# A two-layer graph kernel on one Trainium2 core: four second-layer tiles of each batch computed as halves, with copies loaded by GpSimd's queue, and the bias added by a DMA

## The reference

```python
# layer 0, attention
h = einsum('bnf,fo->bno', x, W)
e = h @ a1 + swapaxes(h @ a2, 1, 2);  e = where(e >= 0, e, 0.2 * e)
attention = softmax(adj * e, axis=1)
x1 = einsum('bij,bjo->bio', attention, h) + bias[None] + x
# layer 1, graph convolution with batch norm
support = einsum('bnd,df->bnf', x1, W1) + b1
y = einsum('bnm,bmf->bnf', adj, support)
y = (y - mean) * rsqrt(var + 1e-5) * gamma + beta     # mean, var over batches and nodes
out = relu(y) + x1
```

## Time and profile before

| | |
|---|---|
| Time, median of 3 runs | 909.66 us (909.13 to 911.93) |
| The profiled execution, its own time | 911.96 us |
| Its span, first to last instruction | 910.2 us |
| Mean granted clock of TensorE | 0.984 |
| PE busy | 871.0 us (96%) |
| ACT busy | 804.2 us (88%) |
| DVE busy | 726.1 us (80%) |
| POOL busy | 211.6 us (23%) |
| DMA, mean over the span | 271 GB/s, 246.39 MB |

### The profile page before, as it was taken

The page is one execution under the profiler, slowest core; times in us unless marked ns, Lnnn a source line. Parts: engine busy times, 40 slices in busy tenths (PEclk is TensorE's granted clock), DMA queues, the critical chain, the costliest instruction groups (busy, mean ns, idle before and its releaser), DMA issues.

```text
span 910.2 us, 8919 instructions
## 1 busy us (share of the span) xinstructions
PE 871.0 (96%) x3167; PEld 547.5 (60%) x3167; DVE 726.1 (80%) x794; ACT 804.2 (88%) x614; POOL 211.6 (23%) x166
## 2 busy tenths in 40 slices
PE   6999999999999999999999999999999999999960
PEld 4335556675656756676566756567566765666850
DVE  3655788797878888887877978788888978879966
ACT  5998699988999799998999889997999979997645
POOL 0012214250333112341142401341113411323000
PEclk9999999999999999999999999999999999999995
DMA  8996676748677595867767495775957677565988
GB/s 337 422 362 240 260 291 237 292 165 334 224 273 268 203 360 173 294 234 267 280 237 300 155 357 207 267 274 199 358 174 292 231 263 287 192 224 190 423 335 344
DMA packets 46220, 246.39 MB, mean 271 GB/s; under 512 B 5560, under 2 KB 6184, under 8 KB 19552
## 3 DMA queue, kind: packets, MB, share of 16 engines
q1 hardware_dynamic: 46176, 245.82, 71.7%
HBM read 221.57 MB, written 24.23 MB: 270 GB/s over the span
## 4 chain that ended last, share of the span: by engine, by line
PE 83%; DVE 7%; ACT 3%; issue 2%; DMA 2%; SPq 1%; POOL 0%; DVEq 0%; ACTq 0%; POOLq 0%
PE acc L526 40%; PE acc L499 10%; PE acc L493 10%; PE acc L495 10%; DVE exp_lo L765 4%; PE acc L480 4%; PE acc L507 2%; PE acc L454 2%; PE acc L539 1%; PE acc L542 1%; PE acc L541 1%; ACT scores L623 1%; DMA adj_slot<-biasT 1%; DVE stats L786 1%; ACT hi L637 1%
## 5 line engine op out<-in xcount | busy, mean ns | idle before, releaser
L746 DVE CUSTOM_DVE_ANT_0 scores<-scores,adj_slot 128x2048 f32<-128x2048 f32 x128 | 297.5, 2324 | 77.5 <-ACT scores L616 30.2
L765 DVE SCALAR_TENSOR_TENSOR exp_lo<-scores,rz,hi 128x2048 fp32r<-128x2048 f32 (+1 forms) x133 | 280.5, 2125 | 0.0
L616 ACT ACTIVATE scores<-adj_slot,f_cols 128x2048 f32<-128x2048 f32 x128 | 255.0, 1998 | 15.4 <-PE acc L499 11.8
L623 ACT ACTIVATE scores<-scores,neg_mx 128x2048 f32<-128x2048 f32 x128 | 255.1, 1993 | 14.2 <-DVE neg_mx L749 14.2
L637 ACT ACTIVATE hi<-scores,rz 128x2048 fp32r<-128x2048 f32 (+1 forms) x133 | 227.5, 1726 | 33.6 <-DVE rz L758 30.4
L526 PE MATMUL acc<-adj_slot,region_even 128*128 128x512 f32 x512 | 228.8, 592 | 0.0
L526 PE MATMUL acc<-adj_slot,region_odd 128*128 128x512 f32 x392 | 175.3, 592 | 0.8 <-DVE region_odd L801 0.8
L526 PEld LDWEIGHTS acc<-adj_slot,region_even 128*128 128x128 f32 x512 | 96.7, 190 | 99.7 <-issue 95.7
L499 PE MATMUL acc<-exp_lo,h_hi 128*128 128x512 f32 x448 | 121.5, 391 | 0.8 <-DVE exp_lo L765 0.7
L526 PEld LDWEIGHTS acc<-adj_slot,region_odd 128*128 128x128 f32 x392 | 74.0, 190 | 77.2 <-issue 73.2
L495 PE MATMUL acc<-hi,h_hi 128*128 128x512 f32 x448 | 119.9, 390 | 0.0
(11 more groups left out here) (77 smaller groups left out, 614.7 us busy)
## 6 DMA issues: line engine op xcount, KB each, us to landing
adj_slot<-adjT SPq DMA_DIRECT2D x159, 1024.0 KB, 5.1
adj_slot<-xT SPq DMA_DIRECT2D x20, 1024.0 KB, 7.6
adj_slot<-biasT SPq DMA_DIRECT2D x32, 256.0 KB, 6.5
xp_dram<-adj_slot SPq DMA_DIRECT2D x32, 256.0 KB, 2.6
adj_slot<-xp_dram SPq DMA_DIRECT2D x8, 1024.0 KB, 12.1
adj_slot<-f_rows SPq DMA_DIRECT2D x7, 1024.0 KB, 6.9
adj_slot<-y_dram SPq DMA_DIRECT2D x7, 1024.0 KB, 12.0
outT<-adj_slot SPq DMA_DIRECT2D x6, 1024.0 KB, 4.7
```

The source lines that it names most:

```text
L616: act.activation(scores[t % ER][:, :], slots[f1_slot(bt.par)][:, :], ACT.Prelu, bias=f2_cols[:, bt.n, t:t + 1], alpha=ALPHA).then_inc(edge ...
L623: act.activation(scores[e][:, :], scores[e][:, :], ACT.Exp, bias=neg_mx[:, e:e + 1], accum_out=zsum[:, e:e + 1]).then_inc(exp_done, 1)
L746: dve.tensor_tensor_reduce(scores[e][:, :], scores[e][:, :], slots[s][:, :], 1.0, NEG_BIG, ALU.mult, ALU.max, mx[:, e:e + 1]).then_inc(max ...
L765: dve.scalar_tensor_tensor(exp_lo[e][:, part_cols(t, i)], scores[e][:, part_cols(t, i)], rz[:, e:e + 1], hi[m][:, part_cols(t, i)].bitcast ...
```

## The change

1. **Four layer-1 tiles of a batch in halves.** For k = 3, 7, 10 and 14 of batches 1 to 6, and k = 10 and 14 of batch 0, PE runs `layer1_halves`: twelve float32r matmuls in the place of four float32 ones. A float32r copy of the adjacency tile comes by a DMA on POOL's queue (`load_hi`), into a slot that is free for a while; DVE subtracts it from the tile in place (`tile_low`); ACT and DVE split the 128 support columns (`part_high`, `part_low`).
2. **Slots.** Tiles 2, 3, 4 swap slots with tiles 9, 11, 10 from batch to batch (`SWAP`), so the next batch's tiles 2, 3 and 4 are loaded around the batch's end (`load_early`) and not after layer 1's k = 0, 1 and 2. The slots of tiles 2 and 3 hold copies after their score and are loaded again for layer 1 (`LENT`, at k = 7 and 10): two more 1 MB loads a batch. The four old reloads come at k = 3, 4, 5, 6 and not at k = 1, 2, 3, 4.
3. **The bias.** One DMA on POOL's queue adds the bias (1 MB) onto the residual in SBUF, in the place of four loads of it by SP and four adds on POOL. The residual is loaded one k earlier, at k = 12.

```diff
-    T_F, T_BIAS, T_X, T_RES = 8, 9, 10, 11
+    T_F, T_HI, T_X, T_RES = 8, 9, 10, 11
+    SWAP = {2: T_HI, 3: T_RES, 4: T_X}
+    HI_AT = {3: T_F, 7: 2, 10: 3, 14: T_HI}
+    LOW_STEP = {3: 1, 7: 5, 10: 8, 14: 11}
+    RELOAD = {T_F: 3, T_HI: 4, T_X: 5, T_RES: 6}
+    K_HI = max(k for k in HI_AT if HI_AT[k] == T_HI)
+    FIRST_HI = [10, 14]
+    LENT = {u: max(k for k in HI_AT if HI_AT[k] == u) for u in HI_AT.values() if u not in (T_F, T_HI)}
...
                     for k, t in enumerate(SIGMA):
                         wait_l1(sp, pv, k)
-                        if t >= PRE:
+                        if t >= PRE and k > 2:
                             load_adj(bt, t)
...
-                        if k == T_BIAS + 1:
-                            load_bias(bt)
+                        if k == T_RES + 1:
+                            load_residual(bt)
...
+                if not is_last(bt):
+                    load_early(nx, 2)
+                    load_early(nx, 3)
                 store_xp(bt)
+                if not is_last(bt):
+                    load_early(nx, 4)
...
+            def layer1_halves(bt, k):
+                t = SIGMA[k]
+                tile_hi = slots_lo[hi_slot(bt, k)]
+                pe.wait_ge(part_lo_done, split_no(bt, k))
+                pe.wait_ge(hi_loaded[k], hi_value(bt, k))
+                for c in range(NC):
+                    pe.matmul(acc1[c][:, :], part_lo[bt.par][:, tile_cols(t)], tile_hi[:, cols(c)], start=False, stop=False)
+                for c in range(NC):
+                    pe.matmul(acc1[c][:, :], part_hi[:, :], tile_hi[:, cols(c)], start=False, stop=False)
+                pe.wait_ge(tile_lo_done, split_no(bt, k))
+                for c in range(NC):
+                    mm = pe.matmul(acc1[c][:, :], part_hi[:, :], slots_lo[l1_slot(bt, t)][:, cols(c)],
+                                   start=False, stop=False)
+                mm.then_inc(l1_tile, 1)
...
# ScalarE, step t, after exp(bt, t)
+                    for k in (() if is_first(bt) else halved(bt.n - 1)):
+                        if LOW_STEP[k] == t:
+                            part_high(bt.prev(), k)
...
# VectorE, step t, after score(bt, t + 1), recip(bt, t), exp_low(bt, t - 1)
+                        if LOW_STEP[k] == t:
+                            tile_low(bt.prev(), k)
+                            part_low(bt.prev(), k)
...
# GpSimd
-                pool.wait_ge(bias_loaded[c], 16 * (bt.n + 1))
-                pool.tensor_tensor(res_sb[:, cols(c)], res_sb[:, cols(c)], bias_sb[:, cols(c)], ALU.add)\
-                    .then_inc(xb_done, 1)
+                pool.dma_start(res_of(bt)[:, :], biasT, accum_op=ALU.add).then_inc(xb_done, 16)
...
+                    split_h(bt, 0)
+                    split_h(bt, 1)
+                    halves_of(pv, 7, load_hi)
+                    split_h(bt, 2)
+                    halves_of(pv, 10, load_hi)
+                    split_h(bt, 3)
+                    split_h(bt, 4)
+                    halves_of(pv, 14, load_hi)
...
+                add_bias(bt)
+                if not is_last(bt):
+                    halves_of(bt, 3, load_hi)
```

More of the change, by code:

```diff
@@ L205, in adj_value, with again_value, hi_slot, split_no @@
                 return 16 * (bt.half + 1)
-            return 16 * (bt.n + 1 + (t in STAGED))
+            return 16 * (bt.n + 1 + (slot_of(bt.par, t) in STAGED))
         def l1_slot(bt, t):
-            if t == T_F and not is_last(bt):
+            if t in (T_F, T_HI, T_RES, T_X) and not is_last(bt):
                 return slot_of(1 - bt.par, t)
             return slot_of(bt.par, t)
+        def again_value(bt, t):
+            return 16 * (bt.n + (t not in LENT))
+        def hi_slot(bt, k):
+            if HI_AT[k] == T_F:
+                return l1_slot(bt, T_F)
+            return slot_of(1 - bt.par, HI_AT[k])
+        def split_no(bt, k):
+            return sum(len(halved(n)) for n in range(bt.n)) + halved(bt.n).index(k) + 1
+        def halved(n):
+            return FIRST_HI if n == 0 else list(HI_AT)
+        def hi_value(bt, k):
+            return 16 * (bt.n + (k in FIRST_HI))
         def part_cols(t, i):
@@ L561, in step @@
                         while ahead < min(t + (LEAD if t > 0 else LEAD - 1), NT):
-                            layer1(bt.prev(), ahead)
+                            if ahead in halved(bt.n - 1):
+                                layer1_halves(bt.prev(), ahead)
+                            else:
+                                layer1(bt.prev(), ahead)
                             ahead += 1
@@ L657, in support_high, with part_high @@
                     act.copy(sup_hi[:, cols(c)], region[bt.par][:, cols(c)]).then_inc(sup_hi_done, 1)
+            def part_high(bt, k):
+                t, j = SIGMA[k], halved(bt.n).index(k)
+                act.wait_ge(sup_out, NC * bt.n + t // TC + 1)
+                if j > 0:
+                    wait_l1(act, bt, halved(bt.n)[j - 1])
+                elif bt.n > 0:
+                    wait_l1(act, bt.prev(), halved(bt.n - 1)[-1])
+                act.copy(part_hi[:, :], region[bt.par][:, tile_cols(t)]).then_inc(part_hi_done, 1)
             def h_from_psum(bt, banks):
@@ L907, in split_h, with load_hi, add_bias, halves_of @@
                                    ALU.subtract).then_inc(h_lo_done, 1)
-            def add_bias(bt, c):
+            def load_hi(bt, k):
+                nx = bt.next()
+                if HI_AT[k] == T_F:
+                    pool.wait_ge(edge_out, NT * (bt.n + 1))
+                else:
+                    pool.wait_ge(max_done, NT * nx.n + HI_AT[k] + 1)
+                    for u in HI_AT:
+                        if u < k and HI_AT[u] == HI_AT[k]:
+                            wait_l1(pool, bt, u)
+                pool.dma_start(slots_lo[hi_slot(bt, k)][:, :], adjT[bt.n, tile_cols(SIGMA[k]), :])\
+                    .then_inc(hi_loaded[k], 16)
+            def add_bias(bt):
                 pool.wait_ge(res_loaded, 16 * (bt.n + 1))
-                pool.wait_ge(bias_loaded[c], 16 * (bt.n + 1))
-                pool.tensor_tensor(res_sb[:, cols(c)], res_sb[:, cols(c)], bias_sb[:, cols(c)], ALU.add)\
-                    .then_inc(xb_done, 1)
+                pool.dma_start(res_of(bt)[:, :], biasT, accum_op=ALU.add).then_inc(xb_done, 16)
+            def halves_of(pv, k, also):
+                if k in halved(pv.n):
+                    also(pv, k)
             def step(bt):
```

109 lines of the change are left out of this document (67 added, 42 removed).

## The result

| | before | after |
|---|---|---|
| Time, median of 4 runs of each on one chip | 909.98 us (909.13 to 911.93) | 901.75 us (899.29 to 903.24) |
| Ratio | | 0.990, 95% interval 0.988 to 0.992 |
| The profiled execution: time, span | 911.96, 910.2 us | 902.67, 900.9 us |

What follows compares the result with a forecast made beforehand. PE's own instruction stream was taken as the bound (busy 106.14 of a 106.31 us stage). Halved tiles -18.7, new waits +1.2 and batch 0 +1.5 gave -16.0, so 909.66 became 893.7 us; range 889 to 907.

Steps and rivals of the forecast that it cites:

- Halved tiles, -18.7: PE, layer 1: twelve float32r matmuls take 2.72 us, not 3.44, saving 0.72 on each of 26 tiles: -18.7 us.
- DVE's room for the first subtraction: DVE, batch start: loading tile 2 early removes 2.89 us of idle, leaving 2.2 us of room before PE wants the halves.
- thinnest cover of all: ACT, full batches: four casts of 0.3 us make it 99.2 of 103.4 us busy; ordinary steps win back the loss; no price.
- ACT or DVE takes over: Rival, chance 0.2: ACT's 0.64 us loss per halved tile is never won back, 907.6 us; half won back, 900.
- DMA engines the bound: Rival, chance 0.08: copies, reloads and bias fill the DMA engines, so the kernel gets slower, 930 us at R = 3.5.
- R: DMA engines: times as long POOL's queue's bytes hold them as plain bytes; full at 3.0, old batch length passed at 3.2.
- hidden, for anything under 19 us: Bias DMA, batch end: taken as 8 us, issued from 492.5 on, needed by 511.5 for the support, so no cost.
- Loads in general: Tiles 5 and up: a landing may take 9.1 us, 8.4 with a halved tile between; it takes 5.1, cover enough.
- New waits, +1.2 (bounds 0 and 6): PE, full batches: moments where DVE's room of some 1 us isn't enough, 0.2 us a batch, at most 1 us.
- Batch 0, +1.5 (-1.4 to 3.6): Batch 0's boundary: bias follows the residual, landing at 89.7 to 94.6; support ends 1.4 us earlier to 3.6 later: +1.5 us.
- What would show it wrong: Signs: copies or bias over 15 us to land, loads' median landing over 8 us, or PE waiting for `hi` at batch end.
- the forecast proper: Whole kernel: the case "as forecast", 889 to 898 us, with chance 0.68.

Runs made afterwards that it cites:

- Experiment 7: Experiment 1's kernel with the next batch's tile 2 loaded after k = 0 again, tile 4 still loaded early: 956.09 us, ratio 1.046 to the kernel before.
- Experiment 9: Experiment 1's kernel with tiles 2 and 4 both loaded late, after k = 0 and k = 2, tile 3 still early: 922.61 us, ratio 1.012 to before.
- Experiment 1: The changed kernel with the load of x for h moved from k = 12 to k = 14, behind tile 15's: 895.44 us, ratio 0.982 to before.
- Experiment 8: The changed kernel with the residual back at k = 13, behind tile 15, x for h staying at k = 12: 894.94 us, ratio 0.981 to before.
- Experiment 3: The changed kernel with the accumulating bias DMA cut to 128 of 2048 columns, the other bias left out: 895.32 us, ratio 0.982 to before.
- experiment 5: Experiment 1's kernel with batch 0's loads ordered tile 0, f1, residual, tile 1, and tile 2 after the bias: 890.75 us, ratio 0.976 to before.

## Why the prediction was half right, step by step

- **Halved tiles, -18.7.** Right: 2.72 us from start to start, and 0.71 a tile from the two floors (26 x 0.71 = 18.5).
- **DVE's room for the first subtraction.** Right in mechanism. The 2.89 us of idle are gone, the 128-column subtraction takes 0.48 us here (0.28 to 0.83 over the 26) and not 0.27, and the low half of the support is ready 2 us before PE takes it. The whole tile's subtraction takes 2.57 us in the mean and not 2.28, so DVE's new work is 3.1 us a halved tile and not 2.55, without a wait of PE for it in this stage. Experiments 7 and 9 show that all of this hangs on the early load.
- **ACT, the "thinnest cover of all", no price.** Right: 98.99 us busy in a stage of 102.99 without a gap on PE. The rival "ACT or DVE takes over" fell: its number (900 with half of the gain lost) is close to the result, its cause isn't.
- **DMA engines the bound.** Fell. With R as there, plain bytes at 384 GB/s, the copies have R = 1.1 and the bias R = 1.8. The forecast's 3.2 for both came from 425 GB/s; with the 384 of the kernel after the old length would be passed at R = 2.4, still above both. The page "DMA: Bandwidth & Descriptors" of the Trainium skill (section "Specifications") gives about 358 GB/s of HBM per core. The kernel before exceeded it for 20 us (425 GB/s); over a whole stage nothing here tests it, since a stage needs only 326.
- **The bias, "hidden, for anything under 19 us".** True of the support, which it was checked against: the bias took 11.8 us in the median, and nothing waited for it after batch 0. But that step asked only who waits for this DMA, and not what it does to a load in flight beside it.
- **"Loads in general", the step that failed.** It let a landing take 9.1 us (8.4 with a halved tile) and then used 5.1 us, the median of before. Both sides were wrong for tile 15, and either alone would have done no harm. Its room is 6.2 us: from tile 15's issue (486.98) to the undisturbed start of its layer 0 (504.07) are 17.1 us, for no layer-1 tile stands in PE's last two steps. The chain behind the landing is the score, negation and reciprocal of 14 (2.56), `hi` of 14 (1.92), the exponential (1.98), copies of y (1.90) and four quarters of `hi` (2.46), together 10.8, which leaves 6.3. The stages bear this out. The landings of tile 15 in the five stages after batch 0's are 7.8, 7.4, 8.3, 8.0 and 8.4 us, and these stages are 1.6, 1.2, 2.0, 1.8 and 2.2 us over 102.95: each is late by what its landing has over 6.2. I followed only DVE's low half behind the score, not the reciprocal that is queued behind it and the whole of ACT after that. And the load took 8.25 us, because "the residual is loaded one k earlier" puts it together with x for h ahead of tile 15, and its bias DMA right behind. The excess makes the 1 to 2 us by which a stage is over its floor. Experiments 1 and 8 each remove it by moving one load by one or two k.
- **New waits, +1.2 (bounds 0 and 6).** Measured +7.7, over the bound.
- **Batch 0, +1.5 (-1.4 to 3.6).** The mechanism was right, and the landing came within its bounds (90.3, or 92.3 with the 2 us by which this timeline runs ahead of that of before; 89.7 to 94.6 were given). The size was +3.7 in one trace, just over the upper bound, since 1.6 us of clock after the wait weren't counted, and +0.95 in the other. Experiment 3 removes it; experiment 5's trace has none of it, but experiment 1's, with the old order, has only 0.45.
- **What would show it wrong.** "If PE waits for `hi` at the end of a batch" was the sign that came, and PE's waits were not under 3 us in all. The other two signs did not come: the bias landed in 11.8 us and the copies in 5.9 in the median, and the loads of tiles in 6.8.

16.0 us forecast, less 6.5 of waits and 2.2 of batch 0 that were missed, is 7.3; medians gave 8.2. That the range of 889 to 907 held is in part luck: the forecast proper, 889 to 898 with a chance of 0.68, was missed, and the range reached 901.75 only because of rivals whose causes did not come.

Still open: what the median of the bias DMA alone hides, how much of experiment 5's gain is its order of loads, and the start, which scatters by 3 us among kernels that differ only behind it. In the two traces of the change 1.4 us of its 2 us stand in one gap of PE at 21 us (0.99 and 0.98 us, where it is 2.40 before and in experiment 1).

## What to carry to other kernels

When a load is moved, list every transfer in flight at its new place and follow the chain behind each of *their* landings through all in-order queues (here score, next to it a reciprocal, then ACT), at the last steps of a stage first, where the pattern of the steps ends. A median landing time is no price for a load in a burst. When a change gives half of what its arithmetic says, compare the stages' lengths with the one stage that lacks one of the loads; then move single loads, for the cure may be one line (ratio 0.990 to 0.981 here, and 0.978 with batch 0's order too). And take a boundary's cost from more than one trace: here it was 3.7 us in one and 0.95 in the next.
